# A decoder layer on one core: split q and k of the second group get buffers of their own, values are projected at other units, fours of attention as two pairs

## Chip, cores and metric

One core of one Trainium2 chip runs the whole program in one launch. The metric is device time in microseconds (us). The kernel before took 810.05 us, the median of three runs (809.73 to 810.14).

## The reference

`x` is 8 batches of 512 tokens with 256 channels. Three residual steps:

```python
x = x + attention(layernorm(x), Wq, Wk, Wv, Wo)      # causal over tokens, 16 heads of 32 (16 real + 16 imaginary)
x = x + cross(layernorm(x), ctx, ctx)                # per token: 16 heads against 16 heads, causal over heads
x = x + ffn(layernorm(x), kernel, bias, a, b)        # kernel rounded to int4 steps, plus a low-rank a @ b
```

All is in float32. In the first step `scores = q k / sqrt(16)`, a softmax over the keys, `out @ Wo`. In the second, for each token and head h, the softmax runs over heads k <= h of the context of the same token.

## The kernel before, in words

**Tiling.** The 16 heads of a batch are four groups of four heads (g = 0 to 3). A group's q and k are projected on TensorE with split float32r operands (`project_qk`, L578: high and low parts, six matmuls of 512 columns for q, six for k). ScalarE copies the high part to `q_hi`, `k_hi` (L978), VectorE takes the low part to `q_lo`, `k_lo` (`low_part`, L1227), and SyncE issues six transfers of 256 KB each (L456, `stack`) that put head, low and high parts under each other in `stack_q` and `stack_k`, one of four slots. Only then can scores be computed.

**Units.** Each group's scores are computed twice, in ten units of up to 512 columns: once with queries on the partitions, for the row maxima (`max_bank`, VectorE reduces each, `take_max`, L1214), and once with keys on the partitions and the maxima folded in as a 97th row, for the exponentials (`exp_bank`, ScalarE, L950, into a ring `probs` of five units). The exponentials then go into `attend` (L619): for units 0 to 3 (at n = 5), units 4 to 7 (at n = 9), and units 8 and 9 as a pair at n = 1 of the next group. Its matmuls have 32 columns of weights; head h writes column strip h of `acc_bank`, and the sums of the probabilities go to strip h + 2 of `sum_bank`.

**Stages.** Every engine runs the same nest written out by hand: batch i (from -1), group g, unit n. In turn (i, g) the group C = g is exponentiated, the maxima of the group two ahead (B) are taken one unit late, the group three ahead (A) is projected at n = 1 and 2, and at n = 1 the maxima of the group one ahead (M) are transposed (`turn_maxima`, L639, into PSUM bank `misc[1]`), copied to `max_row` by ScalarE (L968) and sent by ScalarE's own DMA queue as the 97th row (L970). Batches 3 to 5 are a hardware loop, the others are written out.

**The two misc banks.** q uses `misc[0]`, k `misc[1]`; the transpose of the maxima, ScalarE's inverse sums (L1002), the output projection, the values and the FFN share them. `take` (L511) makes TensorE wait for the last reader of the bank.

**Values.** `project_v` (L587) computes the values of two groups for half of the tokens, 12 matmuls of 256 columns, at n = 0 (half 0, bank 1) and n = 5 (half 1, bank 0) of g = 0 and g = 2; `keep_values` (L923) on ScalarE copies them at n = 1 and n = 5. A pair's values are first used two turns after the projection of its half 0, at n = 5.

**The start.** In (-1, 1) the first group is projected, in (-1, 2) (`FIRST_PASS`) the values, the second group, and then the first group's maxima; in (-1, 3) and (0, 0) (`stack_early`, L396) the third and fourth group are projected at n = 1 before that turn's first maximum. ScalarE waits for all transfers of the stack before (L977) ahead of overwriting `q_hi`. `keep_busy` (L527) adds idle matmuls there.

**Cross attention** runs beside it, one tile of 128 tokens per turn: GpSimd multiplies (L315 and L1603), VectorE sums: `score_sums` at n = 5 and 8, `value_sums` (L1245) at n = 0. At g = 1 VectorE also adds the output projection to x1 (`add_to_x1`, L1259: half 0 at n = 0, half 1 at n = 1) and takes the layernorm's statistics. ScalarE normalises x at n = 5 and 6 of g = 3, x1 at n = 5 and 6 of g = 1, x2 at n = 2 and 3 of g = 0 (L910).

## Time and profile before

| | |
|---|---|
| median of 3 runs | 810.05 us (809.73 to 810.14) |
| the profiled execution | 811.71 us |
| its span, first to last instruction | 809.9 us |
| TensorE busy | 746.5 us, 92% |
| VectorE busy | 601.1 us, 74% |
| GpSimd busy | 493.0 us, 61% |
| ScalarE busy | 401.2 us, 50% |
| DMA moved | 70.55 MB |

Busy time is that of matmuls, or of the instruction's own execution; register, branch, semaphore and DMA-issuing instructions aren't counted. PE is TensorE, ACT ScalarE, DVE VectorE, POOL GpSimd, SP SyncE; PEld are TensorE's weight loads. A wait is shown as `[us <- who ended it]`. A row of stretches gives start:end, length, then busy us and instructions of PE, PEld, DVE, ACT and POOL, the granted TensorE clock (1.00 is 2.4 GHz), the DMA engines' mean busy share (over 1.00 where packets overlap) and GB/s. `misc<-ident,neg_max` is the transpose of the maxima; `head_out` are the value sums. Matmuls are pipelined, so their durations overlap: the time one costs is that from its start to the next one's.

### The profile page before, as it was taken

Reading aid. Unit: us, or ns where it says so; the run is one execution under the profiler, and the core shown is the slowest. Engines: PE = TensorE matmul, PEld = TensorE weight load, DVE = VectorE, ACT = ScalarE, POOL = GpSimd, SP = SyncE. Lnnn points to the kernel's source line nnn. Section 1 sums busy time; section 2 is a strip of 40 time slices with the busy share of each in tenths; the row PEclk is TensorE's granted clock in tenths of the full one; section 3 lists DMA queues with packets and bytes.
Section 4 is the critical chain, followed back from the end, with each engine's and each line's share of the span. In section 5 each row is a group of like instructions: output and inputs, shape, how many; then the busy total and the mean of one; then the engine's idle time right before and its main releaser. Section 6 shows DMA issues by size and latency. Waiting matters only on the chain.

```text
span 809.9 us, 16213 instructions
## 1 busy us (share of the span) xinstructions
PE 746.5 (92%) x5733; PEld 528.2 (65%) x5733; DVE 601.1 (74%) x1227; ACT 401.2 (50%) x760; POOL 493.0 (61%) x458
## 2 busy tenths in 40 slices
PE   8788999999998999999999989999999999898996
PEld 6555565755575656666666757675766565478996
DVE  3544555457768896889778886888787959699984
ACT  5123555455555556555736564656565555552111
POOL 5000000031975889687958796879867896986763
PEclk9998999999999999999999999999999999999999
DMA  5886666866686668567756775677666770100101
GB/s 186 111 109 105 79 80 86 137 86 87 86 137 79 92 87 136 68 86 115 91 99 84 112 91 93 84 116 93 97 86 101 97 112 8 60 8 14 34 14 39
DMA packets 47981, 70.55 MB, mean 87 GB/s; under 512 B 4897, under 2 KB 22578, under 8 KB 47922
## 3 DMA queue, kind: packets, MB, share of 16 engines
q1 hardware_dynamic: 46898, 69.52, 57.4%
q8 instruction: 35, 0.57, 0.3%
q10 hardware_dynamic: 1024, 0.26, 0.2%
q14 instruction: 24, 0.20, 0.1%
HBM read 14.98 MB, written 4.19 MB: 24 GB/s over the span
## 4 chain that ended last, share of the span: by engine, by line
PE 63%; DVE 13%; DMA 10%; ACT 7%; issue 4%; POOL 1%; SPq 1%; ACTq 0%; DVEq 0%; POOLq 0%
PE misc L525 19%; PE exp_bank L525 16%; PE max_bank L525 10%; DMA stack_k<-k_lo 9%; PE acc_bank L525 8%; PE sum_bank L525 7%; DVE neg_max L1225 3%; DVE head_out L1237 3%; ACT probs L950 2%; ACT x_in L910 1%; PE misc L575 1%; ACT values L903 1%; SPq L456 1%; DVE prod L360 1%; PE misc L642 1%
## 5 line engine op out<-in xcount | busy, mean ns | idle before, releaser
L950 ACT ACTIVATE probs<-exp_bank 128x512 f32<-128x512 f32 x320 | 185.9, 594 | 202.8 <-PE sum_bank L525 109.6
L1225 DVE TENSOR_REDUCE neg_max<-max_bank 128x1 f32<-128x512 f32 (+1 forms) x192 | 130.2, 683 | 108.9 <-PE max_bank L525 107.9
L1603 POOL TENSOR_TENSOR prod<-head_probs,ctx_sb 128x256 f32<-128x256 f32 (+1 forms) x100 | 181.8, 1851 | 2.2 <-POOL head_probs L1598 0.5
L525 PE MATMUL max_bank<-stack_k,stack_q 96*128 96x384 f32 (+3 forms) x512 | 155.2, 364 | 15.0 <-DMA stack_k<-k_lo 8.1
L525 PE MATMUL exp_bank<-stack_q,stack_k 97*128 97x384 f32 (+3 forms) x512 | 149.8, 354 | 15.8 <-ACT probs L950 14.9
L315 POOL TENSOR_TENSOR prod<-x1n,ctx_sb 128x256 f32<-128x256 f32 (+1 forms) x104 | 158.2, 1553 | 4.6 <-ACT x1n L910 4.6
L1537 POOL TENSOR_TENSOR ln_var<-ln_mv,eps 128x4 f32<-128x4 f32 x21 | 4.5, 212 | 198.1 <-DVE ln_mv L1211 198.1
L525 PEld LDWEIGHTS exp_bank<-stack_q,stack_k 97*128 97x128 f32 x512 | 83.3, 192 | 48.3 <-ACT probs L950 23.2
L1225 DVE TENSOR_REDUCE seg_max<-max_bank 128x4 f32<-128x512 f32 x128 | 86.8, 684 | 37.5 <-PE max_bank L525 36.5
L525 PEld LDWEIGHTS max_bank<-stack_k,stack_q 96*128 96x128 f32 x512 | 85.8, 198 | 22.5 <-DMA stack_k<-k_lo 9.8
L525 PE MATMUL acc_bank<-probs,values 128*32 128x512 f32 (+3 forms) x1024 | 96.4, 447 | 0.9 <-ACT probs L950 0.9
L525 PE MATMUL sum_bank<-probs,ones 128*32 128x512 f32 (+3 forms) x1024 | 94.4, 439 | 0.0
L525 PE MATMUL exp_bank<-mask_k,ident_b 128*128 128x256 bf16 (+1 forms) x320 | 84.5, 264 | 0.0
L525 PE MATMUL max_bank<-mask_q,ident_b 128*128 128x256 bf16 (+1 forms) x320 | 84.4, 264 | 0.0
L1237 DVE TENSOR_REDUCE score_rows<-prod 128x64 f32<-128x1024 f32 (+1 forms) x104 | 79.7, 808 | 5.5 <-POOL prod L315 5.5
L1237 DVE TENSOR_REDUCE head_out<-prod 128x64 f32<-128x256 f32 (+2 forms) x100 | 74.8, 810 | 1.5 <-POOL prod L1603 1.5
L525 PE MATMUL exp_bank<-prod,ident 128*128 128x160 f32 (+4 forms) x416 | 62.8, 313 | 3.5 <-POOL prod L360 2.4
L525 PEld LDWEIGHTS exp_bank<-prod,ident 128*128 128x128 f32 x416 | 60.5, 195 | 5.5 <-POOL prod L360 2.7
L525 PEld LDWEIGHTS sum_bank<-probs,ones 128*32 128x32 f32 x1024 | 33.8, 111 | 37.1 <-issue 32.5
L525 PE MATMUL misc<-xt_hi,w_hi 128*128 128x512 f32 x128 | 55.4, 432 | 2.0 <-DVE xt_lo L1334 1.2
L525 PEld LDWEIGHTS exp_bank<-mask_k,ident_b 128*128 128x128 bf16 x320 | 31.1, 97 | 36.1 <-issue 27.0
L1616 POOL TENSOR_TENSOR head_probs<-score_rows,head_max 128x256 f32<-128x256 f32 x26 | 16.3, 628 | 61.5 <-DVE head_max L1352 61.4
(183 smaller groups left out, 1372.6 us busy)
## 6 DMA issues: line engine op xcount, KB each, us to landing
stack_q<-q_hi SPq DMA_DIRECT2D x64, 256.0 KB, 5.0
stack_k<-k_hi SPq DMA_DIRECT2D x64, 256.0 KB, 9.5
stack_q<-q_lo SPq DMA_DIRECT2D x32, 256.0 KB, 7.0
stack_k<-k_lo SPq DMA_DIRECT2D x32, 256.0 KB, 10.7
x_in<-in_x SPq DMA_DIRECT2D x9, 512.0 KB, 6.0
ctx_sb<-in_ctx SPq DMA_DIRECT2D x32, 128.0 KB, 3.1
x<-in_x SPq DMA_DIRECT2D x7, 512.0 KB, 10.3
out<-y_sb SPq DMA_DIRECT2D x5, 512.0 KB, 3.2
```

What stands on the lines that cost most here:

```text
L315: last = engine.tensor_tensor(qk_prod[:, COFF[j]:COFF[j + 1]].rearrange("p (q k d) -> p q k d", q=4, d=HD), x1n[:, t, 4 * j * HD:4 * (j + ...
L360: last = engine.tensor_tensor(end_prod_qk[:, d0:d1, COFF[j] // HD:COFF[j + 1] // HD].rearrange("p d (q k) -> p d q k", q=4), end_x1n_turne ...
L456: sp.dma_start(to[n * D:(n + 1) * D, s, :, :].bitcast(F32), part[:, :].bitcast(F32)).then_inc(stacked, 16)
L525: return nc.tensor.matmul(*args, **kw)
L575: last = nc.tensor.transpose(bank[:, t * P:(t + 1) * P], src[:, t, c * P:(c + 1) * P], ident[:, :])
L642: nc.tensor.transpose(bank[0:G * NT, 0:P], neg_max[:, slot % 2, :, :].rearrange("p h t -> p (h t)"), ident[:, :]).then_inc(max_psum, 1)
L903: return nc.scalar.activation(dst, src, ACT.Identity)
L950: nc.scalar.activation(probs[:, (UNITS * g + n) % PTR, :], exp_bank[n % 2][:, :], ACT.Exp, scale=SCALE).then_inc(exp_done, 1)
L1225: vec.tensor_reduce(o, v, axis=AX_X, op=ALU.max, negate=True).then_inc(max_taken, 1)
L1237: last = vec.tensor_reduce(out(j), products(j), axis=AX_X, op=ALU.add)
L1603: last = gp.tensor_tensor(pv_prod[:, COFF[j]:COFF[j + 1]].rearrange("p (q d k) -> p q d k", q=4, k=keys), head_probs[:, 4 * j:4 * j + 4, N ...
L1616: gp.tensor_tensor(head_probs[:, :, :], head_scores[:, :, :], head_max[:, :, None].to_broadcast([P, NH, NH]), ALU.subtract).then_inc(h_shi ...
```

## The change

1. **Buffers.** The second group's split parts go to four buffers of their own (three pieces of `pv_prod`, one of `y_sb`, both unused so early), with an own semaphore `second_stacked`. ScalarE doesn't wait for the first stack ahead of them.
2. **Third group.** It is projected in `FIRST_PASS` at n = 4, ahead of that unit's maximum, not in (-1, 3). Its split uses the old buffers.
3. **Values.** `values_due`: g = 0 half 0 at n = 3, half 1 at n = 5; of the pair of g = 2, half 0 at g = 2, n = 3 and half 1 at g = 3, n = 5. Both halves use bank 0. ScalarE's copies move likewise.
4. **Pairs.** `attend` for four units becomes two calls of two units.
5. **VectorE at g = 1.** `add_to_x1(1)` comes ahead of all value sums; the sums move from n = 0 to n = 1 (chunks 3 and 2) and n = 2 (chunks 0 and 1).

```diff
+        second_stacked = sem("second_stacked")
...
+        def values_due(i, g, n):
+
+            at = {0: (0, {3: 0, 5: 1}), 2: (2, {3: 0}), 3: (2, {5: 1})}.get(g)
+            if not at or n not in at[1] or (i, at[0]) == FIRST_PASS:
+                return None
+            pair, half = values_pair(i, at[0]), at[1][n]
+            return (pair[1], half) if pair else None
...
+        THIRD_SPLIT = 4
+        first_split = (q_hi, q_lo, k_hi, k_lo)
+        second_split = [pv_prod[:, (n + 2) * T:(n + 3) * T].bitcast(F32R) for n in range(3)]
+        second_split.append(y_sb[:, 0:2, :].rearrange("p a c -> p (a c)").bitcast(F32R))
...
+                        second = (i, g) == FIRST_PASS
+                        sp_q_hi, sp_q_lo, sp_k_hi, sp_k_lo = second_split if second else first_split
+
                         def stack(to, n, part):
                             sp.dma_start(to[n * D:(n + 1) * D, s, :, :].bitcast(F32),
-                                         part[:, :].bitcast(F32)).then_inc(stacked, 16)
+                                         part[:, :].bitcast(F32)).then_inc(second_stacked if second else stacked, 16)
...
             def project_v(pair, half):
 
-                bank = take(1 - half, v_ready, r_v)
+                bank = take(0, v_ready, r_v)
...
-                        if stack_early(i, g) and n == 1 and (i, g) != FIRST_PASS:
-                            if i >= 0:
-                                turn_maxima(st["M"][1])
+                        if (i, g) == FIRST_PASS and n == THIRD_SPLIT:
+                            for which in (0, 1):
+                                project_qk(2, which)
+                        if (i, g) == (0, 0) and n == 1:
+                            turn_maxima(st["M"][1])
                             for which in (0, 1):
                                 project_qk(st["A"][1], which)
...
-                            if unit == 0:
+                            if unit == 0 and (i, g) == (-1, 3):
+                                pe.wait_ge(second_stacked, 16 * STACK_DMAS)
+                            elif unit == 0:
                                 pe.wait_ge(stacked, n_stack.up(16 * STACK_DMAS))
...
                             if n in (5, 9):
-                                attend(range(n - 5, n - 1), st["C"][1], first_tile)
+                                for pair in ((n - 5, n - 4), (n - 3, n - 2)):
+                                    attend(pair, st["C"][1], first_tile)
...
-                        if values_pair(i, g) and n in (0, 5) and (i, g) != FIRST_PASS:
-                            project_v(values_pair(i, g)[1], n // 5)
+                        if values_due(i, g, n):
+                            project_v(*values_due(i, g, n))
...
-                     misc[1 - half][:, :].rearrange("p (t s n) -> p s t n", t=2, s=2)).then_inc(v_ready, 1)
+                     misc[0][:, :].rearrange("p (t s n) -> p s t n", t=2, s=2)).then_inc(v_ready, 1)
...
-                        if values_pair(i, g) and n == 1 and (i, g) != FIRST_PASS:
-                            keep_values(values_pair(i, g)[1], 0)
...
-                        if st["A"] and n in (1, 2):
+                        if (i, g) == FIRST_PASS and n in (1, 2):
                             act.wait_ge(qk_psum, n_qk.up())
                             n_lo.up()
-                            if n == 1:
+                            copy(second_split[2 * (n - 1)], misc[n - 1][:, :]).then_inc(qk_hi_ready, 1)
+                        third = (i, g) == FIRST_PASS and n in (THIRD_SPLIT, THIRD_SPLIT + 1)
+                        if third or (st["A"] and n in (1, 2) and (i, g) not in (FIRST_PASS, (-1, 3))):
+                            which = n - (THIRD_SPLIT if third else 1)
+                            act.wait_ge(qk_psum, n_qk.up())
+                            n_lo.up()
+                            if which == 0:
 
                                 wait(act, stacked, n_staged.up(16 * STACK_DMAS) - 16 * STACK_DMAS)
-                            copy((q_hi, k_hi)[n - 1][:, :], misc[n - 1][:, :]).then_inc(qk_hi_ready, 1)
+                            copy((q_hi, k_hi)[which][:, :], misc[which][:, :]).then_inc(qk_hi_ready, 1)
...
-                        if values_pair(i, g) and n == 5 and (i, g) != FIRST_PASS:
-                            keep_values(values_pair(i, g)[1], 1)
+                        if values_due(i, g, n):
+                            keep_values(*values_due(i, g, n))
...
-                        if stack_early(i, g) and n == 1:
+                        if (i, g) == FIRST_PASS and n in (1, THIRD_SPLIT):
+                            for which in (0, 1):
+                                low_part(which, second_split if n == 1 else first_split)
+                        if (i, g) == (0, 0) and n == 1:
                             for which in (0, 1):
                                 low_part(which)
...
-                        if added and n == 0:
+                        late_sums = g == 1 and ok(i - 1)
+                        if late_sums and n == 1:
+                            add_to_x1(1)
+                        if added and n == (1 if late_sums else 0):
                             dve.wait_ge(hpv_prod, n_pv.up())
...
-                        if g == 1 and ok(i - 1) and n == 1:
-                            add_to_x1(1)
...
-                        if added and n == 0:
+                        if added and n == (1 if late_sums else 0):
                             value_sums((2,))
-                        if added and n == 0:
+                        if added and n == (2 if late_sums else 0):
                             value_sums((0, 1)).then_inc(hpv_sum, 1)
```

## Rows read from the trace of the kernel before

**Rows 1.** the page, part 1: busy us, share of the span, instructions

```profile
PE 746.5 (92%) x5733; PEld 528.2 (65%) x5733; DVE 601.1 (74%) x1227; ACT 401.2 (50%) x760; POOL 493.0 (61%) x458
```

**Rows 2.** the wait table of the whole span: us in total, times, longest

```profile
PE misc L642 <- ACT values L903: 13.1, 15, 1.3
...
PE max_bank L525 <- DMA stack_k<-k_lo: 8.1, 7, 2.6
...
PE misc L642 <- DVE x L1262: 4.7, 7, 0.7
```

**Rows 3.** the chain of waits, 0 to 75 us: start, us, what

```profile
20.95 10.93 DMA stack_k<-k_lo
...
61.98 0.58 PE max_bank L525 x2
```

**Rows 4.** SyncE's queue in order of time: start, us, transfer, how many

```profile
17.57 1.33 SPq L456 DMA_DIRECT2D stack_q<-q_hi  x2
...
32.66 1.19 SPq L456 DMA_DIRECT2D stack_q<-q_hi  x2
...
459.52 1.21 SPq L456 DMA_DIRECT2D stack_q<-q_hi  x2
```

**Rows 5.** stretches at the start: busy us by engine, PEclk, DMA share, GB/s

```profile
27.50:30.00 2.50, 1.79 (x17) 1.37 (x14) 0.00 (x0) 0.00 (x0) 0.00 (x0) 1.00 1.09 126
30.00:32.00 2.00, 0.07 (x1) 0.07 (x1) 0.00 (x0) 0.03 (x1) 0.00 (x0) 1.00 0.16 17
```

**Rows 6.** the row of maxima: ScalarE's issue, and landing times of all 32

```profile
43.06 0.60 ACTq L970 DMA_DIRECT2D stack_q<-max_row  x1
...
DMA to landing us min/median/max: 1.8/1.8/5.1
```

**Rows 7.** a stretch of two us in (0, 0), columns as in rows 5

```profile
66.00:68.00 2.00, 2.00 (x9) 1.50 (x9) 0.99 (x2) 0.60 (x1) 0.00 (x0) 0.50 1.08 128
```

**Rows 8.** four stretches between transposes of maxima, batches 4 and 5, from g=1

```profile
416.79:437.06 20.27, 18.93 (x150) 12.24 (x150) 18.08 (x38) 12.74 (x25) 13.92 (x14) 1.00 0.64 84
437.06:457.06 20.00, 20.00 (x166) 14.13 (x167) 15.85 (x35) 10.03 (x19) 14.16 (x12) 1.00 0.71 108
457.06:476.20 19.14, 17.45 (x146) 11.24 (x142) 18.88 (x40) 11.79 (x23) 17.73 (x18) 1.00 0.69 93
476.20:502.40 26.20, 24.77 (x182) 17.91 (x182) 18.61 (x34) 14.05 (x26) 22.00 (x16) 1.00 0.65 105
```

**Rows 9.** TensorE in order of time, batch 4: instructions that had waited

```profile
381.48 0.51 PE L525 MATMUL exp_bank<-stack_q,stack_k 97*128 97x256 f32 x2 [0.48 <-ACT probs L950]
...
390.59 0.28 PE L642 MATMUL misc<-ident,neg_max 128*16 128x128 f32 x1 [0.74 <-ACT values L903]
...
396.51 0.50 PE L525 MATMUL exp_bank<-stack_q,stack_k 97*128 97x384 f32 x2 [0.76 <-ACT probs L950]
...
416.79 0.28 PE L642 MATMUL misc<-ident,neg_max 128*16 128x128 f32 x1 [0.67 <-DVE x L1262]
...
422.84 0.50 PE L525 MATMUL max_bank<-stack_k,stack_q 96*128 96x384 f32 x2 [0.40 <-DVE neg_max L1225]
```

**Rows 10.** VectorE in order of time, g=1 of batch 4

```profile
412.55 2.99 DVE L1237 TENSOR_REDUCE head_out<-prod 128x64 f32<-128x1024 f32 x4
...
419.23 0.69 DVE L1225 TENSOR_REDUCE neg_max<-max_bank 128x1 f32<-128x512 f32 x1 [1.83 <-PE max_bank L525]
```

**Rows 11.** the chain (a four, then values), and TensorE (a pair, then the transpose)

```profile
107.39 1.00 PE acc_bank L525 x8
108.38 0.86 PE sum_bank L525 x8
109.24 1.62 PE misc L525 x12
...
456.04 0.65 PE L525 MATMUL acc_bank<-probs,values 128*32 128x256 f32 x8
...
457.06 0.28 PE L642 MATMUL misc<-ident,neg_max 128*16 128x128 f32 x1
```

More of the change, by code:

```diff
@@ L453, in body @@
                         wait_apart(sp, const_ready, (exp_scored, n_free.up(UNITS) - UNITS * SLOTS))
+                        second = (i, g) == FIRST_PASS
+                        sp_q_hi, sp_q_lo, sp_k_hi, sp_k_lo = second_split if second else first_split
                         def stack(to, n, part):
                             sp.dma_start(to[n * D:(n + 1) * D, s, :, :].bitcast(F32),
-                                         part[:, :].bitcast(F32)).then_inc(stacked, 16)
+                                         part[:, :].bitcast(F32)).then_inc(second_stacked if second else stacked, 16)
                         wait_apart(sp, const_ready, (qk_hi_ready, n_hi.up()))
-                        stack(stack_q, 0, q_hi)
-                        stack(stack_q, 2, q_hi)
+                        stack(stack_q, 0, sp_q_hi)
+                        stack(stack_q, 2, sp_q_hi)
                         wait_apart(sp, const_ready, (qk_lo_ready, n_lo.up()))
-                        stack(stack_q, 1, q_lo)
+                        stack(stack_q, 1, sp_q_lo)
                         wait_apart(sp, const_ready, (qk_hi_ready, n_hi.up()))
-                        stack(stack_k, 0, k_hi)
-                        stack(stack_k, 1, k_hi)
+                        stack(stack_k, 0, sp_k_hi)
+                        stack(stack_k, 1, sp_k_hi)
                         wait_apart(sp, const_ready, (qk_lo_ready, n_lo.up()))
-                        stack(stack_k, 2, k_lo)
+                        stack(stack_k, 2, sp_k_lo)
                     if g == 0 and ok(i - 1):
@@ L1225, in take_max, with low_part @@
                 vec.tensor_reduce(o, v, axis=AX_X, op=ALU.max, negate=True).then_inc(max_taken, 1)
-            def low_part(which):
+            def low_part(which, parts=first_split):
                 dve.wait_ge(qk_hi_ready, n_hi.up())
-                hi, lo = ((q_hi, q_lo), (k_hi, k_lo))[which]
+                hi, lo = parts[2 * which:2 * which + 2]
                 vec.tensor_tensor(lo[:, :], misc[which][:, :], f32(hi[:, :]),
```

## The prediction

> **What bounds the kernel now.** I read the engines' busy shares first: TensorE is busy 92% of the span [rows 1], so only its waits can be won, or work moved into them. The wait table then names two of them at one place, the transpose of the maxima: 13.1 us in 15 waits for ScalarE's copy of the values, 4.7 us in 7 waits for VectorE's addition to x1 [rows 2]. Both hold PSUM bank 1, which the transpose wants.
>
> Next the chain of waits over the first 75 us. Here the bound is not TensorE but the transfers that stack q and k: 10.93 us from the last issue to the landing [rows 3], and the like for each of the next two stacks. A stack is issued at 17.57 and landed at 31.88, so 14.3 us; the next one only then starts, at 32.66 [rows 3, 4], because it reuses the split buffers. The reader is to see that the DMA engines are full (1.09) up to 30 us and nearly idle (0.16) from 30 to 32 [rows 5].
>
> Last, the steady loop: one batch is four stretches from one transpose of the maxima to the next, 20.27 (g=1 to 2) + 20.00 (g=2 to 3) + 19.14 (g=3 to 0) + 26.20 (g=0 to 1) = 85.61 us [rows 8]. No stretch with a stack in it can be shorter than 2.46 us (transpose to issue, 457.06 to 459.52) + 14.3 (landing) + 0.5 (first scores) + 1.01 (the pair, 456.04 to 457.06 with the transpose behind it) = 18.2 us [rows 3, 4, 11]. That floor is a term below.
>
> **Part by part: the start.** The second group's own buffers take away the wait at 31.88. Its split is then ready once its projection is, at about 27 (its two values halves now share bank 0, which puts it back by about 1 us; hidden, since the queue is full to 30). So the second stack follows the first without a gap. A stack is 1.57 MB, and at the 126 GB/s of the row at 27.5 [rows 5] that is 12.4 us: first ends near 30.4, second 42.8, landing some 1.4 us after its last data (0.16 of the stretch from 30 to 32 was busy, so to about 30.4 of 31.88), 44.1. The third is projected amid the first maxima (2.8 us of TensorE, which waits for VectorE there), so it is issued from about 37 and is queued too: data to 55.1, landing 56.5. Before, its first scores start at 61.98 [rows 3]. TensorE has to be there at 56.6: the third's low parts now stand before the fourth maximum on VectorE and put the first transpose of maxima back by some 2.5 us, to 44.9. The second group's maxima (7 us) then end at 52, the transpose is at 53.8, the projections (2.8) end at 56.6. So both arrive together: gain 5.4. But the values' first half of (0,0) moves from unit 0, where TensorE waited anyway, to unit 3, where it doesn't: +1.5 us (12 matmuls, 1.62 with their tail [rows 11]). Net at the next transpose: **−3.9**.
>
> The clock: at 66 to 68 the row has 0.50, that is 1.2 instead of 2.4 GHz [rows 7], after TensorE had been mostly waiting between 56 and 66. Work there runs twice as long for some 6 us. In the new kernel the waits before it are shorter (projections fill 53.8 to 56.6). Bounds: 0, or all of it, about 3; I take **−2**, since only the waits before VectorE's first maxima stay.
>
> **The row of maxima** goes out on ScalarE's queue while two stacks are in flight. Its landing took 1.8 us in the median, 5.1 at worst [rows 6], and the worst is the first, issued at 43.06 into a full queue. Between "after the transfer in progress" (2 us) and "after the whole backlog" (to 55.1) the row doesn't decide, as only 2 us of backlog were left then. I take the first: it lands near 48.5, and is wanted at 52. The Trainium skill (DMA: Bandwidth & Descriptors, "Queues, rings and completion order") states that each DMA engine goes round robin between the queues by packets. By that rule the row costs nothing here; by the other reading the sum loses 4 us, and that stays a rival.
>
> **Values.** They leave unit 0 of g=0 and g=2. In 15 of these the transpose waited for their copy; a stretch of g=0 loses 0.74 [rows 9], in all 13.1 us [rows 2]. But the 1.5 us of matmuls come back elsewhere:
> - g=0, unit 3: TensorE waits 0.76 (0.95 counted start to start) for an exponential there [rows 9], as ScalarE is normalising; the values fill it. Net +0.6 for batches 3 and up, +1.5 for batches 0 to 2, which have no such wait.
> - g=2, unit 3 in, unit 5 out: 0. q's low part is free just in time.
> - g=3, unit 5: the wait of 0.48 for an exponential [rows 9], and its like one unit later, look like cover, and aren't. ScalarE has the layernorm of x queued behind the values' copy, and the copy waits for the 1.5 us of matmuls; its exponentials come as much later. +1.6.
> So 19.14 becomes 19.14 − 0.8 − 1.5 + 1.6 = 18.4, hardly above the floor: −0.8. In batches 0 to 2 and 6, whose stretches I read in the same way, the floor of 18.2 is already touched (7 waits of the maxima's scores for the stack, 8.1 us [rows 2]): there −0.9 to −1 is what the transpose's wait gives, and no more.
>
> **The late sums (g=1).** VectorE's addition moves ahead of 2.99 us of value sums that began at 412.55, in VectorE's wait for the scores [rows 10]. It can't start before the first maximum, which needs scores that end at 415.1. So the transpose comes at 416.4 instead of 416.79: −0.4. The sums now fall into the 1.83 us that VectorE had free before 419.23 [rows 10] (2.1 us of them fit) and the last two (1.0 us) lie before the third maximum; TensorE, which waits for that one until 422.84 [rows 9], goes on at 423.65, +0.8. From there TensorE and VectorE run abreast, and nothing is caught up. With v gone from the unit 0 behind (−1.5) and its wait (−0.9): 20.27 becomes 19.05. Together with g=0 (26.2 − 0.4 + 0.6 = 26.4), g=2 (0) and g=3 (−0.8): **−1.8 per batch**, where the waits at hand (some 0.8 before the transposes of g=0, 1 and 2, and 0.95 in g=0) would promise −3.4.
>
> In the last batch's g=1 nothing is projected, so there is no 1.83 us to take the sums: +2.
>
> **Fours as two pairs.** A four takes 1.00 + 0.86 us, eight matmuls abreast in time, a pair 1.01 [rows 11]. A split four keeps all four column strips filled (scores' sums lie two strips over), so I take 0. The first pair frees its probabilities 0.9 us sooner; ScalarE starts earlier, but TensorE's waits on it are mostly those of g=0 and g=3 above. −1 in all. Lower bound of the cost 0; upper, if each split costs what a pair costs over half a four (1.01 − 0.93 = 0.08): 64 × 0.08 = 5.
>
> **Sum.** Start −3.9, clock −2. Rest of batch 0: two stretches −1 each = −1.9. Batch 1 (g=0, 1, 3; its late sums have nothing to sum yet): +0.9 − 1.3 − 0.9 = −1.3. Batch 2: +1.15 − 1.8 − 0.9 = −1.55. Batches 3 to 5: −5.4. Batch 6: +0.2 − 1.3 − 1 = −2.1. Batch 7: +0.2 + 2 = +2.2. Pairs −1. Total −17.0, and the profiled execution (811.71) becomes 794.8. It stood 1.66 above the median of 810.05; against the median the sum gives 793.1. I round to **794**.
>
> **Rivals.**
> 1. The row of maxima waits behind the backlog. Batch 0 then starts at 56.5 instead of 52, the third group's scores at 60.6: 4 us are lost, and TensorE idles 4.5 us, so the clock's 2 too: 800. For it: the 5.1 us row. Chance 0.17.
> 2. VectorE is worse off: all 3 us of sums end up before TensorE's third maximum in each g=1 (+2.2 instead of +0.8, 6 times) and it lags into g=2: 794 + 8 = 802. For it: VectorE is busy 18.08 of 20.27 us there [rows 8]. Against: the 1.83 us are free. Chance 0.13.
> 3. Slower: the split fours. The wait between two pairs keeps the second from filling strips that the first leaves, and each pair drains. It decides from 16/64 = 0.25 us a split; if the pairs ran only two strips abreast, a four would take 1.86 more, and 64 of them make +119, so 912; with a drain of 0.3, 64 × 0.3 = 19, so 813. Against: the pair at hand takes 1.01, not 1.9. Chance 0.06.
> 4. No overlap: the two stacks in flight share the DMA engines so that nothing lands earlier than the third does now; the start gives nothing and the loop's gains alone are left (794 + 5.4): 799. Chance 0.07.
> 5. Better: the clock never falls and ScalarE's earlier exponentials pay in g=3 (1 for the clock, 0.7 in 7 batches): 788. Chance 0.10.
>
> **How the numbers follow.** My forecast (790 to 798) has 0.47. The range takes in rivals 1, 2, 4 and most of 5 and the unknown cost of the splits (+5): 786 to 804. 0.2% is 1.6 us, about what a measurement of this kernel tells from no change. Faster 0.90, within 0.03, slower 0.07 (rival 3, and a pile-up of 2 with worse clocks).
>
> **What would show it.** The second stack issued near 27 and landed near 44, the third landed at 56 to 57. No wait of the maxima's transpose for ScalarE's values. In g=1 a wait for VectorE before the third maximum near 1.2 instead of 0.4, and stretches of about 19.0, 20.0, 18.4, 26.4. A granted clock of 1.00 between 60 and 68. Pairs of 0.93 us. It is wrong if fours cost over 1.9, if the batch takes over 84.5 us, or if the first transpose of (0,1) is not near 76.5 (now 82.36).

## The result, and the profile after

The kernel after takes **805.98 us** (median of 20 runs, 803.98 to 811.61), the kernel before beside it 810.69 (20 runs, 809.73 to 816.6): ratio 0.9942, 95% interval 0.9926 to 0.9957. It is faster by 4.7 us, where 17 were forecast; 794 and the range 786 to 804 missed. The profiled execution took 807.63 us, the one before 811.71.

The page, part 1, of the kernel after:

```profile
PE 746.7 (93%) x5733; PEld 529.4 (66%) x5733; DVE 603.2 (75%) x1227; ACT 403.6 (50%) x760; POOL 493.2 (61%) x458
```

Against [rows 1] hardly anything has changed in the work. The mean granted clock has: 0.991 before, 0.975 after (core, span, clock; after). It isn't this one execution: over all 20 executions of the kernel after the clock lies between 0.966 and 0.981, over 61 of the kernel before between 0.982 and 0.994.

```profile
core 0: 805.8 us, clock 0.975
```

Its wait table, TensorE's waits (us in total, times, longest); then two rows of the same table of before that weren't shown:

```profile
PE max_bank L542 <- DVE neg_max L1251: 12.8, 10, 2.2
PE exp_bank L542 <- ACT probs L972: 10.8, 18, 1.0
PE max_bank L542 <- DMA stack_k<-k_lo: 8.5, 8, 2.2
PE exp_bank L542 <- DMA stack_q<-max_row: 3.7, 1, 3.7
PE misc L659 <- DVE x L1288: 3.2, 7, 0.5
```

```profile
PE exp_bank L525 <- ACT probs L950: 14.9, 28, 1.0
...
PE max_bank L525 <- DVE neg_max L1225: 5.0, 9, 1.8
```

Gone are the 13.1 us of waits for the values' copy [rows 2], 1.5 of those for the addition, 4.1 of those for exponentials. New are 7.8 us behind VectorE's maxima and 3.7 in one wait for the row of maxima. The waits became fewer, but some are longer: in batches 3 to 5 none was over 0.80 us before; now each g=1 has one of 1.37 or 1.38.

**The start.** The chain of waits of the kernel after, then SyncE's queue in order of time:

```profile
20.87 11.21 DMA stack_k<-k_lo
...
46.71 9.84 DMA stack_q<-max_row
56.69 0.90 PE exp_bank L542 x2
```

```profile
27.07 1.84 SPq L473 DMA_DIRECT2D stack_q<-prod  x3
...
36.95 1.19 SPq L473 DMA_DIRECT2D stack_q<-q_hi  x2
```

The second stack is issued at 27.07 (forecast 27) and has landed at 44.44 (44.1); the third is issued at 36.95 (37) and has landed at 56.35 (56.5). But the first row of maxima, issued at 46.71, lands after 9.84 us. The DMA engines from 46 to 54 us (packets, then by queue; q1 is SyncE's, q10 ScalarE's):

```profile
DMA packets 576, 1.05 MB, mean 131 GB/s; under 512 B 64, under 2 KB 64, under 8 KB 576
## 3 DMA queue, kind: packets, MB, share of 16 engines
q1 hardware_dynamic: 576, 1.05, 108.0%
```

Not one packet of q10 is among them; the row's packets run from 54.45 on, when the third stack's data are nearly through. TensorE stands, and then runs at half clock (columns as in [rows 5]):

```profile
52.00:54.00 2.00, 0.94 (x6) 0.41 (x4) 1.51 (x3) 0.00 (x0) 0.00 (x0) 1.00 1.06 131
54.00:56.00 2.00, 0.00 (x0) 0.00 (x0) 0.00 (x0) 0.00 (x0) 0.00 (x0) 0.90 0.38 41
56.00:58.00 2.00, 1.31 (x5) 0.94 (x6) 0.00 (x0) 0.38 (x1) 0.00 (x0) 0.50 0.00 0
58.00:60.00 2.00, 1.50 (x6) 0.93 (x6) 0.93 (x3) 0.99 (x3) 0.00 (x0) 0.50 0.00 0
60.00:62.00 2.00, 2.00 (x6) 1.60 (x5) 0.00 (x0) 0.09 (x1) 0.00 (x0) 0.50 0.02 4
62.00:64.00 2.00, 2.00 (x10) 1.42 (x9) 0.69 (x1) 0.60 (x1) 0.00 (x0) 0.89 0.00 0
```

This is the fall of [rows 7], ten microseconds earlier. The first transpose of (0,1) comes at 82.15; before 82.36, forecast 76.5. The new start gives 0.2 us.

**The steady loop.** Four stretches between transposes, batch 5 of the kernel after, from g=1, to be laid beside [rows 8]:

```profile
500.55:518.85 18.30, 16.70 (x138) 10.69 (x139) 18.20 (x38) 12.26 (x24) 11.90 (x13) 1.00 0.70 94
518.85:538.46 19.61, 19.61 (x170) 13.92 (x167) 17.69 (x39) 10.17 (x19) 16.05 (x13) 1.00 0.72 108
538.46:556.87 18.41, 17.23 (x145) 11.18 (x142) 16.80 (x37) 11.78 (x23) 15.97 (x16) 1.00 0.73 101
556.87:583.38 26.51, 25.99 (x197) 19.28 (x194) 19.17 (x33) 14.58 (x27) 24.05 (x18) 1.00 0.58 85
```

82.83 us against 85.61 before and 83.8 forecast: better than forecast. Yet the batches as a whole gained less than forecast, since some stretches look like this (TensorE in order of time, batch 4, g=1; then the stretches around it):

```profile
423.62 0.50 PE L542 MATMUL max_bank<-stack_k,stack_q 96*128 96x384 f32 x2 [1.38 <-DVE neg_max L1251]
...
425.04 1.90 PE L542 MATMUL sum_bank<-probs,ones 128*32 128x512 f32 x4
```

```profile
422.00:424.00 2.00, 0.62 (x6) 0.39 (x4) 1.97 (x5) 0.16 (x1) 1.92 (x4) 1.00 1.09 129
424.00:426.00 2.00, 2.00 (x15) 0.60 (x17) 2.00 (x4) 1.19 (x2) 1.92 (x4) 0.56 1.08 128
426.00:428.00 2.00, 2.00 (x13) 0.35 (x6) 1.35 (x2) 1.57 (x3) 2.00 (x2) 0.59 1.04 124
```

TensorE waits 1.38 us for VectorE, and from 424 the granted clock is at its lower level (1.2 GHz) for some 3.4 us; the four (424.18 to 427.73) then takes 3.55 us instead of 1.85. I call this a **fall**. Reading every trace in stretches of 5 us, a fall loses 1.7 us of clock (5 us times one minus the clock, summed). In time it costs less, since part of the slower work only fills waits: the stretches of the kernel after with a fall take 0.8 to 1.6 us more than like ones without, here or in the traces below (g=1 of batch 4 took 19.57 us, that of batch 3 18.40; g=3 of batch 2 took 20.09, that of batch 3 18.41). Between 75 and 660 us the trace of before has none, that of after six.

The profiled execution was to be 794.8 and is 807.63, so 12.8 us are to be found: the start 5.7 (5.9 forecast, 0.2 found), the last batch's g=1 1.7 (19.03 against 17.4), and between (0,1) and (7,1) 5.6, where 13.05 were forecast and 7.4 came (591.07 to 583.67). These make 13.0; behind (7,2) 0.1 is gained (121.12 to 120.98).

### The profile page after: what moved, and what is told of

It reads as the page before. It is cut to its first block, busy times and chain, and to the rows that moved or that the text cites. A ratio compares the mean times of both kernels' runs of the same rounds, so it can differ in the third digit from the quotient of the medians.

```text
span 805.8 us, 16218 instructions
## 1 busy us (share of the span) xinstructions
PE 746.7 (93%) x5733; PEld 529.4 (66%) x5733; DVE 603.2 (75%) x1227; ACT 403.6 (50%) x760; POOL 493.2 (61%) x458
## 4 chain that ended last, share of the span: by engine, by line
PE 62%; DVE 15%; DMA 12%; issue 4%; ACT 3%; POOL 3%; SPq 1%; DVEq 0%; ACTq 0%; POOLq 0%
PE misc L542 22%; PE exp_bank L542 14%; DMA stack_k<-k_lo 10%; PE max_bank L542 10%; PE acc_bank L542 8%; PE sum_bank L542 7%; DVE head_out L1263 3%; DVE neg_max L1251 2%; DVE ln_raw L1229 2%; DMA stack_q<-max_row 1%; ACT x_in L932 1%; POOL prod L325 1%; DVE prod L370 1%; PE misc L592 1%; ACT probs L972 1%
## 5 line engine op out<-in xcount | busy, mean ns | idle before, releaser
L972 ACT ACTIVATE probs<-exp_bank 128x512 f32<-128x512 f32 x320 | 188.4, 594 | 172.5 <-PE exp_bank L542 101.5
L542 PE MATMUL max_bank<-stack_k,stack_q 96*128 96x384 f32 (+3 forms) x512 | 155.6, 366 | 24.0 <-DVE neg_max L1251 12.8
L542 PE MATMUL acc_bank<-probs,values 128*32 128x512 f32 (+3 forms) x1024 | 152.7, 457 | 0.0
L542 PE MATMUL sum_bank<-probs,ones 128*32 128x512 f32 (+3 forms) x1024 | 150.5, 455 | 0.0
L542 PEld LDWEIGHTS sum_bank<-probs,ones 128*32 128x32 f32 x1024 | 49.0, 112 | 39.2 <-issue 34.6
L542 PE MATMUL exp_bank<-prod,ident 128*128 128x160 f32 (+4 forms) x416 | 61.1, 307 | 3.6 <-POOL prod L370 2.6
L542 PEld LDWEIGHTS exp_bank<-prod,ident 128*128 128x128 f32 x416 | 58.8, 190 | 5.6 <-POOL prod L370 2.8
L542 PEld LDWEIGHTS acc_bank<-probs,values 128*32 128x32 f32 x1024 | 45.7, 112 | 23.4 <-issue 13.8
## 6 DMA issues: line engine op xcount, KB each, us to landing
stack_k<-k_lo SPq DMA_DIRECT2D x31, 256.0 KB, 10.5
```

The source lines that it names most:

```text
L542: return nc.tensor.matmul(*args, **kw)
L972: nc.scalar.activation(probs[:, (UNITS * g + n) % PTR, :], exp_bank[n % 2][:, :], ACT.Exp, scale=SCALE).then_inc(exp_done, 1)
```

## The experiments

My theory after the result, T: the shortfall is the row of maxima, queued behind both stacks, and half clock that follows TensorE's new, longer idle times. The rivals: a part of the change costs time by itself (values, pairs, late sums), or the clock falls whatever TensorE does. Here are all twelve experiments, with 4 to 12 executions each; medians stand beside those of before from the same chip. "Clock" is the mean granted clock of an execution, lowest to highest of all; "(0,1)" is the first transpose there in the profiled execution, "falls" are its falls between 75 and 660 us.

Of the ranges of time that T gave before the runs only r_row_first's was met. c5 came out 0.2 us below its range and s_pairs_only 0.3; c6 missed on the fast side too, the other eight on the slow side. So T is a poor guide to the time, and what holds of it rests on the landings and the clock shown below.

| kernel | us | before | ratio (95%) | clock | (0,1) | falls |
|---|---|---|---|---|---|---|
| before | | | | 0.982–0.994 | 82.36 | 0 |
| after | 805.98 | 810.69 | 0.9942 (0.9926–0.9957) | 0.966–0.981 | 82.15 | 6 |
| s_start_only | 813.19 | 810.47 | 1.0036 (1.0020–1.0053) | 0.985–0.992 | 81.85 | 0 |
| s_values_only | 804.76 | 810.98 | 0.9930 (0.9907–0.9953) | 0.974–0.987 | 83.17 | 2 |
| s_pairs_only | 809.16 | 810.98 | 0.9982 (0.9967–0.9997) | 0.985–0.992 | 80.61 | 0 |
| u_no_late | 806.00 | 810.47 | 0.9942 (0.9922–0.9961) | 0.972–0.983 | 81.47 | 5 |
| r_row_first | 800.64 | 810.47 | 0.9873 (0.9859–0.9888) | 0.977–0.985 | 77.80 | 6 |
| b_busy | 811.54 | 810.47 | 1.0007 (0.9991–1.0024) | 0.969–0.983 | 85.31 | 4, one twice as long |
| c1 | 800.53 | 810.98 | 0.9876 (0.9857–0.9895) | 0.974–0.979 | 78.96 | 5 |
| c2 | 797.59 | 810.98 | 0.9835 (0.9813–0.9857) | 0.983–0.988 | 79.02 | 3 |
| c3 | 796.15 | 811.08 | 0.9801 (0.9768–0.9833) | 0.983–0.988 | 76.73 | 4 |
| c4 | 795.22 | 811.08 | 0.9796 (0.9765–0.9827) | 0.991–0.994 | 75.11 | 2 |
| c5 | 792.29 | 811.30 | 0.9752 (0.9722–0.9781) | 0.991–0.998 | 76.64 | 1 |
| c6 | 795.95 | 811.30 | 0.9800 (0.9771–0.9829) | 0.989–0.991 | 76.80 | 2 |

### The parts, one at a time

**s_start_only**: the kernel before with points 1 and 2 of the change alone (the hunks of `second_split`, `THIRD_SPLIT` and `low_part`).

> The kernel before with the new start alone: the second group's own split buffers and the third group projected amid the first maxima. Values, fours and VectorE's order stay. Theory T: the row of maxima lands at 56 to 57 and the half clock after it eats the gain, so the first transpose of (0,1) is within 1 us of the 82.36 of before, and the total is 809 to 811 (same as before). Rival: it is the values' moves or the late sums that cost the time, and the start gives what I forecast: 804 to 806.

Slower by 2.7 us, and 2.2 above T's range. The row lands at 56.37, the transpose of (0,1) is at 81.85. The 0.5 us that it is ahead there melt to 0.1 by (2, 0), most of it in one stretch of g=3 (19.55 us, 19.28 before). So the start as the change has it is worth nothing or less. Where the 2.7 us come from stays open: the profiled execution has before's span to 0.1 us and shows none of them.

**s_values_only**: before with point 3 alone (`values_due` and bank 0).

> The kernel before with the values' new units and bank alone. Theory T (the values are where the gain of the steady batches comes from, 85.6 to 83.05 without the late sums, and the new start gives nothing as it stands): stretches near 18.4, 19.6, 18.4, 26.7 and a total of 800 to 803, below the 805.98 of the whole change. Rival (forecast: floor and tie of the stretches with all parts): the values alone give about 1.4 a batch, 802 to 806, and the rest needs the late sums.

−6.2 us: as much as the whole change gives or more (the two intervals overlap), so this part carries the gain. It is outside T's range and inside its rival's. Its stretches from g=1 of batch 4 are 18.31, 19.86, 18.57 and 26.66, together 83.4, so 2.2 us less than before; its trace has two falls.

**s_pairs_only**: before with point 4 alone.

```diff
-                                attend(range(n - 5, n - 1), st["C"][1], first_tile)
+                                for pair in ((n - 5, n - 4), (n - 3, n - 2)):
+                                    attend(pair, st["C"][1], first_tile)
```

> The kernel before with the fours as two pairs alone. Both theories: a four takes 1.85 to 1.86 us as before and the time is that of before within 1 us (809.5 to 811.5); ScalarE's exponentials could start 0.9 us sooner behind a four, worth up to -1.5. Rival 3 of the prediction (the pair drains) gives over 813.

−1.8 us. A four takes 1.85 us at full clock (1.86 before), so the split costs nothing. TensorE's waits for exponentials go from 14.9 to 10.5 us, as ScalarE starts earlier, and 3.4 of these 4.4 us come back as waits for the stack (8.1 to 11.5).

**u_no_late**: the kernel after with point 5 undone.

```diff
-                        late_sums = g == 1 and ok(i - 1)
-                        if late_sums and n == 1:
-                            add_to_x1(1)
+                        late_sums = False
...
+                        if g == 1 and ok(i - 1) and n == 1:
+                            add_to_x1(1)
```

> The kernel after with VectorE's order at g=1 as before: the value sums at unit 0, the second half of the addition to x1 behind them. Theory T (the late sums stall TensorE before the third maximum by 1.4 instead of 0.4 us, and the half clock in (2,1), (4,1) and (7,1) follows such stalls): (7,1) goes from 19.0 back to some 15.5 (-3.5), batches 2 and 4 lose their half clock in g=1 (-1 to -1.5 each), the transpose waits for the addition again (+0.5 in six batches). Net -2 to -3: 803 to 804. Rival (my forecast's own reading): the late sums gain 0.4 to 0.9 a batch and cost 2 in (7,1), so nothing changes, 806 to 808.

806.00 against 805.98: the late sums are worth nothing here, as T's rival had it. (7,1) did go back, to 15.15, and the falls in g=1 of batches 2 and 4 are gone, but from batch 1 on g=3 has three (215, 465, 550 us) where the kernel after has one (300). Over all executions the clock is no better, 0.972 to 0.983. So the late sums' long waits aren't needed for the falls. Nor is length alone what decides: this trace has a wait for the stack of 1.2 to 1.4 us in each of batches 2 to 6, and no fall behind any of them. The parts add up: +2.7 −6.2 −1.8 + 0 = −5.3, and the whole gives −4.7.

### The row of maxima

**r_row_first**:

```diff
                         stack(stack_k, 0, sp_k_hi)
+                        if (i, g) == (-1, 3):
+                            sp.wait_ge(max_taken, UNITS + 1)
                         stack(stack_k, 1, sp_k_hi)
```

> The kernel after, but SyncE issues the last two of the third stack's six transfers only after the first row of maxima is out (they wait for the second group's first maximum). Theory T, transfers of all queues go in the order of their issue: only four pieces of the third stack (4 x 2.07 = 8.3 us of data after the second stack's end near 44) stand before the row, so it lands near 52.5 instead of 56.55, TensorE's idle time before (0,0) shrinks from 4 us to under 1, the clock stays at 1.00 around 56 to 62, and the third group's scores start near 59 to 60 instead of 63.67. Total -4 to -6 us: 800 to 802. Rival R1, SyncE's queue is emptied first as long as it holds anything: the row still lands at 56 to 57 and the time stays within 1 us of 806. Rival R2, the queues share by packets: the row would have landed within 2 us already, which the 9.84 us of the kernel after speak against.

800.64, 5.3 below the change. The row lands at 54.32, and its packets now go while q1 still works (q1 and q10 from 47.8 to 54.4 us; then the first scores that need the row):

```profile
q1 hardware_dynamic: 470, 0.86, 107.5%
...
q10 hardware_dynamic: 32, 0.01, 1.6%
```

```profile
54.45 0.47 PE L544 MATMUL exp_bank<-stack_q,stack_k 97*128 97x512 f32 x1 [0.22 <-DMA stack_q<-max_row]
```

TensorE's wait is 0.22 instead of 3.7 us, and the clock doesn't fall there. R1 (SyncE's queue is emptied first) would have kept the row to the end, R2 (sharing by packets) would have let it in within 2 us in both kernels. What fits is the order of issue across the two queues: the row's packets run at 50.54, behind the four pieces issued ahead of it and before SyncE's last two, whose packets end at 56. The DMA engines from 50.5 to 51 us:

```profile
q1 hardware_dynamic: 46, 0.06, 96.8%
q10 hardware_dynamic: 30, 0.01, 18.3%
```

Four pieces' data would put the landing at 52.5. The row's landing comes in 16 parts; 15 of them came between 52.59 and 52.90 and the last at 54.32; in the third stack's pieces that land around it, too, one part comes over a microsecond behind the others.

**c3**: four transfers held back instead of two (on top of c2, below).

```diff
                         stack(stack_q, 2, sp_q_hi)
+                        if (i, g) == (-1, 3):
+                            sp.wait_ge(max_taken, UNITS + 1)
                         wait_apart(sp, const_ready, (qk_lo_ready, n_lo.up()))
                         stack(stack_q, 1, sp_q_lo)
```

> c2 with four instead of two of the third stack's transfers held back until the second group's first maximum. In c2 the row of maxima was issued at 45.59 and landed at 54.05, TensorE stood idle from 51.7 to 54.19 and then ran at half clock from 56 to 59 (the projections took 4.30 instead of 2.82 us). Theory T, transfers of all queues go in the order of their issue: only two pieces (4.1 us of data after the second stack's end near 42.8) stand before the row, so it lands at 50 to 51, TensorE goes on at 51.7 to 52 without idle time, the third group's scores start at 57 to 58 instead of 60.54, and the total is 793 to 795 (c2: 797.59). Rival: with SyncE's issues put off the DMA engines run dry or the third stack lands late (after 58), TensorE waits there instead, and the time is 797 to 798.

796.15; T had 793 to 795. Here the row is issued when the two pieces ahead of it are all but through (SyncE's queue shows the gap; the row's issue is at 47.27, and only four packets of q1 follow until its own at 48.53), and takes 1.85 us:

```profile
38.55 1.19 SPq L474 DMA_DIRECT2D stack_q<-q_hi  x2
48.00 0.55 SPq L474 DMA_DIRECT2D stack_q<-q_lo  x1
```

```profile
53.39 0.48 PE L545 MATMUL exp_bank<-stack_q,stack_k 97*128 97x512 f32 x1
```

No wait for the row stands beside these scores any more, and the projections take 2.82 us instead of c2's 4.30. The transpose of (0,1) is at 76.73; c2 had 79.02. The third group's scores start at 58.26, where 57 to 58 were expected: this execution had a half-clock stretch at 32 to 36 us. The rival is half right: the DMA engines do run dry (a share of 0.04 from 47 to 49), and the third stack lands at 58.05 instead of r_row_first's 56.47. TensorE comes to it at 58.26, so that costs nothing here, by a margin of 0.2 us. c2 and c3 ran on different chips and their intervals overlap, so the 1.4 us between their medians isn't shown by time; the row's landing and the missing wait are.

### The clock

**b_busy**: idle matmuls in TensorE's waits.

```diff
+        IDLE_NEW = {(0, 1): 20, (1, 1): 14}
...
                     if (i, g) == (0, 0):
                         pe.wait_ge(ones_ready, 1)
+                        keep_busy(acc_bank, 36)
...
                             elif unit == 0:
+                                if (i, g) in IDLE_NEW:
+                                    wait(pe, max_taken, n_max_bank.now() - 1)
+                                    keep_busy(max_bank[0], IDLE_NEW[i, g])
                                 pe.wait_ge(stacked, n_stack.up(16 * STACK_DMAS))
```

> The kernel after with idle matmuls (256 columns, 0.107 us each at full clock) in three of TensorE's idle times: 36 ahead of (0,0)'s wait for the row of maxima, 20 and 14 ahead of the waits for the stack at unit 0 of (0,1) and (1,1). Nothing else is changed. Theory T, the half clock after new idle times costs the time: the granted clock stays at 1.00 in 56 to 62, 100 to 105 and 185 to 190, which gives back about 3.2 + 1.7 + 1.3 = 6 us: 799 to 801. Rival: the half clock comes anyway (from the load on the chip, not from idle times): then no gain, 805 to 807.

811.54, outside T's range and its rival's, and half of the miss is my own: the waits for the stack that I had read at 96 and 181 us lie in g=2, not g=1. So the 34 idle matmuls went where TensorE had nothing to wait for and cost 2.2 and 1.5 us. The 36 ahead of (0,0) kept the clock at 1.00 from 54 to 66, but they outlasted the row, and the clock fell at 67 behind the next wait (1.78 us, for VectorE). Here filling one of several waits only moved the fall.

**c1**: r_row_first, with VectorE's order of before in the last batch.

```diff
-                        late_sums = g == 1 and ok(i - 1)
+                        late_sums = g == 1 and ok(i - 1) and ok(i + 1)
...
+                        if g == 1 and i == LAST and n == 1:
+                            add_to_x1(1)
```

> The kernel r_row_first (800.64 us) with one more edit: VectorE's late sums at g=1 only where the turn projects a group, so that (7,1) has the order of before. Theory T: the (7,1) stretch goes from 19.02 to about 15.1 as in u_no_late, nothing before it moves: 796 to 798. Rival: (7,1)'s late end is hidden behind the cross attention of the last tiles, so the total stays at 800 to 801.

800.53 against 800.64: no difference to be measured, as T's rival had it, although (7,1) took 15.16 instead of 19.02. The profiled c1 ends 2.6 us before the profiled r_row_first (798.6 and 801.2), which itself ran 2.3 us above its median. See c6.

**c2**: c1 with idle matmuls in all the new waits up to 190 us.

```diff
+        IDLE_NEW = {(0, 2): 18, (1, 2): 15}
...
+                            if (i, g) == (0, 0) and n == 3:
+                                keep_busy(acc_bank, 18)
...
-                            keep_busy(acc_bank, IDLE_LOW if n == 2 else IDLE_MAXIMA)
+                            third = {5: 12, 6: 10}.get(n) if (i, g) == FIRST_PASS else None
+                            keep_busy(acc_bank, third or (IDLE_LOW if n == 2 else IDLE_MAXIMA))
```

> c1 with idle matmuls where r_row_first's trace has TensorE's new idle times: 12 and 10 behind the maxima's units 4 and 5 of the first pass (waits 1.4 and 1.25 us), 18 ahead of unit 2's maximum in (0,0) (2.06 us), 18 and 15 ahead of the stack's wait at (0,2) and (1,2) (2.4 and 2.1 us); b_busy had the last two a turn too early, where TensorE had nothing to wait for. Theory T: clock 1.00 in 40 to 50, 95 to 100 and 180 to 185, which gives 2 + 1.2 + 1.2 us against c1, so 792 to 794. Rival: the clock falls elsewhere instead (b_busy moved its fall from 55 to 66 us), and the time is c1's within 1 us.

797.59, 2.9 us below c1, of the 4.4 that T expected from the clock (its range of 792 to 794 was missed; the rival: within 1). No fall from 75 to 245 us, where c1 has two and r_row_first three; one did come at 56, behind the wait for the row. The first transpose comes at 44.92, where the prediction had 44.9, though only with idle matmuls that it didn't foresee; and that only made the row wait longer, 8.5 us from issue to landing, which c3 then mended.

**c4**: c3, and

```diff
+                            if g == 1 and ok(i - 1) and n == 5:
+                                wait(pe, exp_done, n_exp_bank.now() - 1)
+                                keep_busy(exp_bank[(n + 1) % 2], 12)
```

> c3 with 12 idle matmuls (1.28 us at full clock) into the free bank of exponentials at unit 5 of every g=1 from batch 1 on, where TensorE waits 1.6 us for VectorE's maximum behind the late value sums. Theory T (the half clock follows TensorE's idle times, so filling this one keeps it up): the half clock behind g=1's first four, 1.5 us each in two or three of the batches of every trace with late sums, is gone: 1.5 to 4 us below c3, 790 to 792. Rival: the wait isn't what brings the clock down, it falls at another place or as often, and the time is c3's within 1 us, or above it where the idle matmuls outlast the wait.

795.22: 0.9 below c3 and far above T's 790 to 792; the intervals overlap, so by time alone the rival isn't out. The clock says more: 0.991 to 0.994 in all five executions, 0.983 to 0.988 in the five of c3 on the same chip. And in the trace g=1's wait is filled,

```profile
411.26 1.48 PE L545 MATMUL exp_bank<-ones 128*128 128x256 bf16 x12
412.68 0.50 PE L545 MATMUL max_bank<-stack_k,stack_q 96*128 96x384 f32 x2
```

and no fall is left in any g=1 (c3 had two, at 245 and 415). That this gives so little time has a reason in the traces: the idle matmuls also cost 0.9 us in (1,1) (19.14 against 18.24) and 0.4 in (7,1). The two falls that remain lie behind g=3's waits for ScalarE, a wait of 0.71 us at 370.80 and one of 0.48 at 372.27 (at this place before it was 0.48, [rows 9], and 0.47):

```profile
370.00:372.00 2.00, 1.08 (x7) 0.71 (x6) 2.00 (x6) 2.00 (x5) 2.00 (x2) 1.00 1.10 130
372.00:374.00 2.00, 1.73 (x14) 1.06 (x18) 1.97 (x10) 0.70 (x2) 1.69 (x1) 0.77 1.06 126
374.00:376.00 2.00, 2.00 (x24) 0.84 (x20) 1.73 (x4) 0.60 (x1) 0.15 (x1) 0.50 0.39 83
```

**c5**: c4, and

```diff
+                            if g == 3 and i >= 1 and ok(i + 2) and n in (8, 9):
+                                wait(pe, max_taken, n_max_bank.now() - 1)
+                                keep_busy(max_bank[(n - 1) % 2], {8: 8, 9: 5}[n])
```

> c4 with idle matmuls in g=3's two waits for ScalarE too, 8 (0.86 us) ahead of the exponentials' scores of unit 8 and 5 (0.53 us) ahead of unit 9, where TensorE waits 0.95 and 0.72 us while ScalarE normalises x, in batches 1 to 5. c4's trace has its two falls of the clock inside the steady batches just behind these waits (1.6 and 1.7 us lost at 373 and 540). Theory T, the falls follow the idle times: none left between 75 and 690 us, 792.5 to 794, less spread between runs. Rival: the falls come anyway, at other places: 795 to 796.

**792.29**, the fastest here: 2.5% below before. On the same chip c6, which has g=3's waits unfilled and late sums in (7,1), took 795.95, and its fastest execution was slower than c5's slowest; 1.2 us of the 3.7 are the late sums (see c6). The clock is 0.991 to 0.998, and the profiled execution is the slowest of the six and has the lowest. One fall is left, at 125 us in (0,3), where nothing is filled. The same place of batch 3 as in c4's rows, now at full clock:

```profile
370.50:375.00 4.50, 4.43 (x38) 3.81 (x37) 3.34 (x7) 3.79 (x8) 4.50 (x3) 1.00 1.07 127
```

From (0,1) to (7,1) it takes 578.15 us, 12.9 less than before; my forecast for that part was 13.05, but without idle matmuls, so that the two agree is in part luck. The idle matmuls do no work of the layer; they cost 0.9 us in (1,1), where batch 1 has no late sums to wait for.

**c6**: c4 with the late sums in the last batch too, so c1's edit taken back.

> c4 with VectorE's late sums in (7,1) too, as the change has them. Theory T: the stretch from (7,1) to (7,2) is 18 to 19 instead of 15.6 us and the end follows, since behind it every trace has the same 121 to 122 us: +3 to +4, 798 to 799. Rival (c1 against r_row_first: 800.53 and 800.64 although c1's stretch was 3.9 us shorter): the end doesn't follow, 795 to 796.

795.95, +0.7 on c4: much less than T's 3 to 4, and where the rival had it. The stretch from (7,1) to (7,2) by kernel, u_no_late, after, c4 and c6 in this order:

```profile
666.45:681.60 15.15, 13.72 (x124) 8.39 (x124) 14.38 (x32) 10.92 (x22) 10.89 (x12) 1.00 0.03 10
```

```profile
665.82:684.85 19.03, 15.96 (x123) 8.88 (x123) 16.41 (x36) 11.20 (x22) 11.23 (x12) 0.82 0.03 8
```

```profile
655.42:671.01 15.59, 14.78 (x135) 9.48 (x135) 13.60 (x32) 11.10 (x22) 11.27 (x12) 1.00 0.04 10
```

```profile
656.42:673.25 16.83, 15.06 (x135) 9.49 (x136) 16.50 (x36) 11.10 (x22) 11.13 (x12) 1.00 0.03 9
```

At full clock the late sums cost 1.2 us there (16.83 to 15.59). The kernel after pays 3.9 because a fall comes on top (clock 0.82). The end does follow: from (7,2) on both take 121 us. c1's missing gain stays unexplained by this; one profiled execution of each can't tell where the others' falls come.

## Why the prediction was wrong

- **The step that failed first** is the row of maxima: "Between 'after the transfer in progress' (2 us) and 'after the whole backlog' (to 55.1) the row doesn't decide ... I take the first: it lands near 48.5". It took 9.84 us and landed at 56.55. Rival 1 had the mechanism (chance 0.17) and put the third group's scores at 60.6; they came at 63.67, since I had priced the clock there at 2 us, and TensorE ran at half speed from 56 to 62. I wrote that the row before "doesn't decide". The packets of that trace would have spoken for rival 1: after the row's issue at 43.06 q1 moved packets alone until 45.20, and the row's came then, as q1's ended. By the rule that I cited (the Trainium skill, DMA: Bandwidth & Descriptors, "Queues, rings and completion order") the row should have got in after one packet of the other queue. Here q1 moved 576 packets in 8 us and q10 none; the measurement decides against using the rule in this way. With the row ahead the transpose of (0,1) is at 77.80 (r_row_first, with a fall at 41 us), and at 76.73 where idle matmuls fill the waits before it too (c3). I had 76.5, so the landings and the work of the start were sized about right; that c3 comes so near is helped by its idle matmuls.
- **The clock was a term of the start only** (−2, "the waits before it are shorter"). In truth there are falls behind waits in the whole kernel after: six between 75 and 660 us, one of twice the length in (7,1), and 5.2 us of clock lost in the start where before has 3.4. The six cost some 7.2 us of time (an estimate: each stretch with a fall against a like one without, of this or another kernel's trace). That is more than the 5.6 us that the batches lack: without falls they would have gained 1.6 beyond the forecast. The one in (7,1) covers the 1.7 of the last batch. I had summed TensorE's idle time and not asked what it does to the clock. That the waits bring the falls is shown by c4 and c5: with waits filled, no useful work removed, the falls go from four to two to one and the granted clock of all executions from 0.983–0.988 over 0.991–0.994 to 0.991–0.998; the median goes from 796.15 to 792.29. Each of the two steps has a pair on one chip: c3 and c4, and c6 (0.989–0.991) and c5. The rival, a clock that falls with the load and not with idle times, is hard to keep beside this, as the idle matmuls add load. What makes one wait bring a fall and a like one not stays open.
- **Values**: right, even modest. No transpose waits for them; stretches of 19.61 and 18.41 (forecast 20.0 and 18.4). Alone they give 6.2 us.
- **The late sums**: the addition did move up (waits 3.2 instead of 4.7 us), and the wait before the third maximum went to 1.38 (forecast 1.2). But g=1's stretch of 18.3 to 18.4 is the same with and without them (u_no_late: 18.35 at 499): it stands on the floor of 18.2 set by the stack, for which TensorE waits 1.25 us there without the late sums. I had 19.05; the 0.8 that I took for lost for good ("nothing is caught up") was caught up. What they gain at the transpose, 0.3 in g=0's stretch (26.35 and 26.66), they lose in (7,1).
- **Pairs**: right. 1.85 us for a four; alone they give 1.8 us where I had 1.
- **Which rivals held**: 1 by its mechanism; 2 and 3 not; 4 (no overlap) not, as the third stack has landed at 56.35; 5 (788) not: even c5, with the row let through and most waits filled, is 4 us from it.

## What to carry to other kernels

Before a stream of transfers is packed closer, look for a small, urgent transfer that will be issued while it runs: on these queues it waited for everything issued ahead of it, from another engine's queue too, and holding back a few pieces of the stream until it was out gave 5 us. Don't add up a busy engine's idle time only; look at the granted clock behind each wait, since a wait here cost another 0.8 to 1.6 us where a fall followed. And take a change apart: here one part (the values) made most of the gain, one (the start) cost 2.7 us by itself, and the repair of the costly one was worth as much as the whole change.

## What the runs showed of the hardware

- A row of 8 KB issued by ScalarE waited for 1.05 MB that SyncE had issued before (9.84 us); with nothing left ahead of it (c3), 1.85 us; with four pieces ahead and two issued behind (r_row_first), 6.51, of which the last 1.4 are those of one part in 16.
- The granted clock falls to its lower level behind some of TensorE's waits. Falls followed waits of 2.20, 1.85 and 1.38 us (kernel after, at 99, 184 and 424 us) and a pair of 0.71 and 0.48 (c4, at 371). They didn't follow each: of the three g=1 waits of 1.4 us in batches 3 to 5 of the kernel after only that of batch 4 had one, and the waits of 0.90 us at the transposes of before had none. The profiled execution differed from its kernel's median by up to 2.6 us (c5: 794.85 and 792.29). The Trainium skill (TensorE: Matmul & The Clock Gate, "Part 1: The HAM clock gate (the "warmup" mystery)") says that the gate is set by how busy TensorE has been, and that the number of slow matmuls at a kernel's start varies from run to run. The traces agree with the first in that filled waits raise the clock (0.984 in c3's median, 0.991 in c4's); the second is seen here behind waits, too (0.966 to 0.981 over the executions of one kernel).
- Matmuls that do nothing, put into a wait, keep the clock up and cost nothing as long as they end before the wait does: in c4 the third maximum's scores start 1.67 us behind the matmul before, 1.42 of it taken by 12 idle ones; in the kernel after, with none, 1.66.
